# One block for attention and the last stage, with the gating of three images run between the attention's score groups

## The chip, the cores and the metric

The kernel runs on one core of a Trainium2 chip. The metric is the device time of one execution in microseconds (us). Before the change it is 2979.22 us (median of 3 runs, 2973.39 to 2980.7).

## The reference, cut to what matters

Four images (B = 4) of 224 x 224 become 56 x 56 patches and a class token: T = 3137 tokens of 128 features. Attention has 8 heads of 16 features and a relative position bias. It is followed by a layer norm, a gate that picks 2 of 8 experts for each image, and the two chosen experts.

```python
h = _L0_tok_ref(x, W, b, cls)                       # (4, 3137, 128)
h = h + _L0_attn_ref(_layernorm(h), Wq, Wk, Wv, Wo, bias_table)
h = h + _L0_ffn_ref(_layernorm(h), attn_w, attn_b, gate_w, gate_b, w1, b1, w2, b2)

# _L0_ffn_ref
scores = x @ attn_w + attn_b
aw = softmax(scores, axis=1)
pooled = sum(x * aw, axis=1)                        # one row for an image
gates = softmax(pooled @ gate_w + gate_b)
_, idx = top_k(gates, 2)                            # two experts for an image
h = gelu(x @ w1[e] + b1[e]);  eo = gelu(h @ w2[e] + b2[e])
```

## The kernel before, in words

The program is a row of blocks with a barrier between them. Tokens are held transposed (128 features on the partitions) and cut into CH = 8 chunks of W = 393 columns.

**First block.** Projections of all images (lines 398 to 460 on TensorE), up to about 213 us. Then attention, whose order is written out by `fast_order` (line 81). One unit is one tile of 128 keys by 393 queries of one of 32 heads (NBH). A head has two sides of four chunks, and one side is a *pass* of 4 x 25 = 100 units; there are 64 passes and 6400 units. Units are put into groups of 4 and 3 in turn. The even group uses PSUM banks 0 to 3, the odd one banks 4 to 6, and bank 7 takes the output. In `scores(g)` (line 466) TensorE waits until ScalarE has exponentiated group g - 2, then makes the score matmuls of the group in f16 (lines 481 and 484), two units beside each other on the rows of the array. ScalarE turns a whole group into exponentials with one instruction (line 575). POOL multiplies the part of a tile near the diagonal by the exponentiated bias (line 620). In `values(m)` (line 487) TensorE multiplies a batch of four units by the value rows in f32 (line 507), four units beside each other on the columns; a batch is issued four groups or more behind its scores and waits for POOL's products. At the end of a pass VectorE copies the output out of bank 7 (line 692), shuffles, takes the reciprocal (697) and multiplies (700). SP stores that half head (line 347), and loads the head after next.

**Second block.** A fallback for large scores, guarded by a flag that every engine loads (lines 819, 909, 927, 1011, 1037). It is skipped with these inputs.

**Third block, the last stage.** Weights are loaded (lines 1263 to 1265), then `gating` runs for each image: output projection (line 1360, the matmul called Y in the change), mean (1340, M), variance (1333, V), square root on ScalarE (1412), reciprocal on VectorE (1472), product (1474), pooling score (1352, S), maximum (1479), exponential (1420), weighted sum (1485), gate logits (1364, G), and the choice of two experts in small VectorE steps. Then `experts` runs 16 units for each image (chunk by expert): four matmuls into the hidden layer (line 1376), Gelu (1436), four matmuls out of it (1384), Gelu (1444), and the weighted add on VectorE (1540). The gating of the next images is laid between the expert units of the current one, from a distance of five slots. Image 0's gating has nothing beside it but the first slots of image 1's. SP loads attention chunks (1273) and expert weights, POOL stores the output (1316).

```python
for g in range(NG + DELAY + 2):
    if g < NG:
        scores(g)
    while done < NB and group_of[batches[done][-1]] + (done % KT == 0) <= g - DELAY - AHEAD:
        values(done)
        done += 1
```

Of the kernel before, what the change touches and what calls it, by code (L numbers as in the profile page):

```python
# [8 lines left out]
F32 = mybir.dt.float32  # L9
# [11 lines left out]
CH = 8  # L21
# [5 lines left out]
REACH = 91  # L27
GMAX = 4
# [29 lines left out]
def at(count):  # L58

    return count + 1  # L60
# [20 lines left out]
def fast_order(NBH, KT):  # L81

    units = [(n, kt, 4 * side + c) for n in range(NBH) for side in range(2) for kt in range(KT) for c in range(4)]
    groups, u = [], 0
    while u < len(units):
        size = GMAX - len(groups) % 2
        groups.append(list(range(u, min(u + size, len(units)))))
        u += size
    batches = [list(range(m, m + 4)) for m in range(0, len(units), 4)]
    return units, groups, batches  # L90


def build(nc, B, S, d):
# [22 lines left out]
    wide_rows = nc.dram_tensor("wide_rows", (HEADS, WIDE), F32, kind="Internal")  # L116
    att_rows = nc.dram_tensor("att_rows", (NBH, CH, 32, W), F32, kind="Internal")

    top = ExitStack()
    with top:  # L120
# [5 lines left out]

        to_prime = []

        def primed(ctx, name, start=1):

            s = semaphore(ctx, name)
            to_prime.append((s, start))
            return s
# [16 lines left out]
        with ctx:  # L152
# [21 lines left out]
            qk_sq = sbuf(ctx, "qk_sq", [P, 2, 2, W], BF16)  # L174
            halves = sbuf(ctx, "halves", [P, 2, 2, 2, W], F16)
# [8 lines left out]
            s_load = semaphore(ctx, "s_load")  # L184
            s_x = [semaphore(ctx, f"s_x{b}") for b in range(B)]
            s_set = semaphore(ctx, "s_set")
            s_h_mm = semaphore(ctx, "s_h_mm")
            s_h = primed(ctx, "s_h")
            s_xc_mm = semaphore(ctx, "s_xc_mm")
            s_wc = semaphore(ctx, "s_wc")  # L190
            s_hsel = semaphore(ctx, "s_hsel")
            s_n2 = semaphore(ctx, "s_n2")
            s_n2k = semaphore(ctx, "s_n2k")
            s_xc = primed(ctx, "s_xc")
            s_sq = semaphore(ctx, "s_sq")
            s_var = semaphore(ctx, "s_var")
            s_std = primed(ctx, "s_std")
            s_rstd = semaphore(ctx, "s_rstd")
            s_ln = primed(ctx, "s_ln")
            s_qk_mm = semaphore(ctx, "s_qk_mm")  # L200
            s_qk_sq = semaphore(ctx, "s_qk_sq")
            s_hi = semaphore(ctx, "s_hi")
            s_lo = primed(ctx, "s_lo")
            s_ln_out = primed(ctx, "s_ln_out")
            s_norm_mm = primed(ctx, "s_norm_mm")
            s_norm = primed(ctx, "s_norm")
            s_v_mm = primed(ctx, "s_v_mm")
            s_v = primed(ctx, "s_v")
            s_v_out = [semaphore(ctx, f"s_v_out{b}") for b in range(B)]
            s_parts_out = [[semaphore(ctx, f"s_parts_out{b}_{i}") for i in range(2)] for b in range(B)]  # L210
            s_band_mm = semaphore(ctx, "s_band_mm")
            s_band = semaphore(ctx, "s_band")
            s_right = semaphore(ctx, "s_right")
            s_shift = semaphore(ctx, "s_shift")
            s_init_out = semaphore(ctx, "s_init_out")
            s_chain = semaphore(ctx, "s_chain")
            s_fl = semaphore(ctx, "s_fl")
            s_fl_mm = semaphore(ctx, "s_fl_mm")
# [44 lines left out]
            s_init = semaphore(ctx, "f_init")  # L263
            s_toep = semaphore(ctx, "f_toep")
            s_e = semaphore(ctx, "f_e")
            s_tick = semaphore(ctx, "f_tick")
            s_ld = [semaphore(ctx, f"f_ld{i}") for i in range(2)]
            s_vld = [semaphore(ctx, f"f_vld{i}") for i in range(2)]
            s_score = semaphore(ctx, "f_score")
            s_exp = semaphore(ctx, "f_exp")  # L270
            s_biased = semaphore(ctx, "f_band")
            s_pv = primed(ctx, "f_pv", BATCHES)
            s_o = primed(ctx, "f_o")
            s_shuf = semaphore(ctx, "f_shuf")
            s_inv = semaphore(ctx, "f_inv")
            s_norm_o = semaphore(ctx, "f_norm_o")
            s_o_out = [primed(ctx, f"f_o_out{i}") for i in range(2)]
# [6 lines left out]
            units, groups, batches = fast_order(NBH, KT)  # L284
# [23 lines left out]
            def batches_until(g):  # L308

                return batch_of[groups[g][-1]] + 1  # L310

# [3 lines left out]
            def _(sp):  # L315
# [78 lines left out]
                for b in range(B):  # L394
                    sp.wait_ge(s_v_out[b], 16)
                    for i in range(2):
                        sp.wait_ge(s_parts_out[b][i], CH * 16)
                for n in range(NBH):
                    store_half(n, 0)
# [4 lines left out]
                for side in range(2):  # L404
                    sp.wait_ge(s_o_out[side], at(16 * NBH))

            @blk.tensor
            def _(pe):
# [57 lines left out]
                def scores(g):  # L466

                    if g >= AHEAD:
                        pe.wait_ge(s_exp, g - AHEAD + 1)
                    for j, u in enumerate(groups[g]):  # L470
# [15 lines left out]
                    last.then_inc(s_score, 1)  # L486

# [24 lines left out]
                for g in range(NG + DELAY + 2):  # L512
                    if g < NG:
                        scores(g)
                    while done < NB and group_of[batches[done][-1]] + (done % KT == 0) <= g - DELAY - AHEAD:
                        values(done)
                        done += 1
                while done < NB:
                    values(done)
                    done += 1  # L520

            @blk.scalar
            def _(act):
# [42 lines left out]

                act.wait_ge(s_toep, 16)
                nc.scalar.activation(e_all[:], e_all[:], ACT.Exp).then_inc(s_e, 1)
                for g in range(NG):
                    act.wait_ge(s_score, g + 1)  # L570
                    if g >= SLOTS_PR:
# [4 lines left out]
                                         ACT.Exp, scale=1.0 / (LIFT * LIFT)).then_inc(s_exp, 1)  # L576

            @blk.gpsimd
            def _(pool):
# [31 lines left out]

                pool.wait_ge(s_e, 1)
                for u in banded:
# [6 lines left out]
                    nc.gpsimd.tensor_tensor(p, p, e_all[0:keys, n % HEADS, t:t + z - a], ALU.mult).then_inc(s_biased, 1)  # L620

            @blk.vector
            def _(dve):
# [63 lines left out]
                for k in range(NBH // 2):  # L687
                    for half in range(4):
                        side = half % 2
                        drained = 4 * k + half  # L690
                        dve.wait_ge(s_pv, BATCHES + k * BATCHES + KT * (half + 1))
                        nc.vector.tensor_copy(o_sb[:, side], ps[:, O_PS, 0:W]).then_inc(s_o, 1)  # L692
                        dve.wait_ge(s_o, at(drained + 1))
                        nc.vector.tensor_copy(tick[:, 0:1], o_sb[:, side, 0:1]).then_inc(s_tick, 1)
                        nc.vector.stream_shuffle(inv[:, side], o_sb[:, side], [HD + i % HD for i in range(32)]).then_inc(s_shuf, 1)
                        dve.wait_ge(s_shuf, drained + 1)
                        nc.vector.reciprocal(inv[:, side], inv[:, side]).then_inc(s_inv, 1)  # L697
                        dve.wait_ge(s_inv, drained + 1)
                        dve.wait_ge(s_o_out[side], at(16 * (2 * k + half // 2)))
                        nc.vector.tensor_tensor(o_norm[:, side], o_sb[:, side], inv[:, side], ALU.mult).then_inc(s_norm_o, 1)  # L700
# [3 lines left out]
        with ctx:  # L704
# [37 lines left out]
            wide_sb = sbuf(early, "z_wide_sb", [HEADS, WIDE])  # L742
            early.close()

# [73 lines left out]
            def _(sp):  # L818
                flag = sp.value_load(flag_i[0:1, 0:1], min_val=0, max_val=3 * HEADS)
                with sp.If(flag > 0):  # L820
                    for dst, src in ((wq2, "Wq"), (wk2, "Wk")):
# [3 lines left out]
                    sp.wait_ge(s_zero2, 1)  # L825
# [81 lines left out]
            def _(pool):  # L907
                prime(pool)
                flag = pool.value_load(flag_i[0:1, 0:1], min_val=0, max_val=3 * HEADS)
                with pool.If(flag > 0):  # L910
                    nc.gpsimd.memset(qg[:, TP:KT * P], 0.0).then_inc(s_pad, 1)
# [14 lines left out]
            def _(pe):  # L926
                flag = pe.value_load(flag_i[0:1, 0:1], min_val=0, max_val=3 * HEADS)
                with pe.If(flag > 0):
                    pe.wait_ge(s_set2, 1)
# [80 lines left out]
            def _(act):  # L1010
                flag = act.value_load(flag_i[0:1, 0:1], min_val=0, max_val=3 * HEADS)
                with act.If(flag > 0):
                    with act.Fori(0, CHUNKS) as n:
# [22 lines left out]
            def _(dve):  # L1036
                flag = dve.value_load(flag_i[0:1, 0:1], min_val=0, max_val=3 * HEADS)
                with dve.If(flag > 0):
                    nc.vector.memset(shift_sb[:, 0:3], 0.0).then_inc(s_zero2, 1)
                    dve.wait_ge(s_w2, 48)  # L1040
# [8 lines left out]
                    with dve.Fori(0, CHUNKS) as n:  # L1049
                        dve.wait_ge(s_zero2, 1)  # L1050
# [98 lines left out]
        with ctx:  # L1149
            wo = sbuf(ctx, "wo", [P, P])  # L1150
            pool_w = sbuf(ctx, "pool_w", [P, 1])
            pool_wr = sbuf(ctx, "pool_wr", [P, P])
            pool_b = sbuf(ctx, "pool_b", [P, 1])
            gate_w = sbuf(ctx, "gate_w", [P, E])
# [426 lines left out]
```

## Time and profile before

| what | us |
|---|---|
| median of the runs (range) | 2979.22 (2973.39 to 2980.7) |
| the profiled execution's own time | 2981.47 |
| its span | 2979.8 |
| projections, until attention's first exponential | 213 |
| attention, first to last exponential (L575) | 2252 |
| from there to the end of the span | 515 |
| mean granted TensorE clock | 0.977 |

PE is TensorE, PEld its weight load, DVE VectorE, ACT ScalarE, SP the queue of most transfers. The table's stages come from the first and last starts of line 575. A row of the timeline gives start, duration, line and operation; "x8" means eight instructions merged, and each f32 matmul of the program leaves two records of MATMUL. Ends of matmuls are modelled, so the distance between two starts is a better measure than a duration. PEclk and "clock" are the granted clock as a share of 2.4 GHz.

### The profile page before, as it was taken

To read this page: it belongs to the slowest core of one execution; us is meant where nothing else is said; L and a number is where in the kernel's file an instruction comes from. 1 tells how busy PE (TensorE), PEld (TensorE's weight loads), DVE (VectorE), ACT (ScalarE), POOL (GpSimd) and SP (SyncE) were. 2 spreads that over 40 slices of the span, in tenths; PEclk is the share of its full clock that TensorE was granted. 3 is DMA by queue.
4 is the path that set the end of the run, shared out by engine and by line. 5 is a ranking of instruction groups with operands and counts; after the bars stand their busy time and mean duration, and the time that the engine had idled before them with its cause. 6 is when DMAs were issued, how large, how long until landed. Compare 5 with 4: busy or idle time off the path is not lost. (4 is left out here: it accounts for less than half of the span.)

```text
span 2979.8 us, 53098 instructions
## 1 busy us (share of the span) xinstructions
PE 2783.5 (93%) x21844; PEld 959.2 (32%) x21844; DVE 633.0 (21%) x798; ACT 2637.8 (89%) x2520; POOL 760.7 (26%) x1421
## 2 busy tenths in 40 slices
PE   7989999999999999999999999999999994799998
PEld 3442222222222222222222222222222221455555
DVE  4751111111111111111111111111111114555441
ACT  4769999999999999999999999999999992467664
POOL 2213332222222333333333322222223330000000
PEclk8989999999999999999999999999999997799999
DMA  5540100000000000000010000000000001110110
GB/s 132 173 156 13 33 29 29 26 26 26 26 28 27 26 26 26 26 26 26 31 34 29 30 29 27 26 26 26 29 26 26 26 7 38 41 42 22 42 33 19
DMA packets 64755, 111.18 MB, mean 37 GB/s; under 512 B 9938, under 2 KB 55084, under 8 KB 63796
## 3 DMA queue, kind: packets, MB, share of 16 engines
q1 hardware_dynamic: 62460, 101.27, 10.9%
q0 software_dynamic: 2048, 6.43, 0.6%
q8 instruction: 178, 2.92, 0.4%
q14 instruction: 69, 0.57, 0.1%
HBM read 62.47 MB, written 46.48 MB: 37 GB/s over the span
## 5 line engine op out<-in xcount | busy, mean ns | idle before, releaser
L575 ACT ACTIVATE shared<-ps 128x1572 f32<-128x1572 f32 (+1 forms) x1829 | 2231.8, 1343 | 20.0 <-PE ps L484 10.0
L507 PE MATMUL ps<-shared,va 128*32 128x393 f32 x12800 | 1433.5, 523 | 0.2 <-DVE flag_i L685 0.2
L620 POOL TENSOR_TENSOR shared<-shared,e_all 128x310 f32<-128x310 f32 (+19 forms) x1344 | 703.5, 537 | 1556.8 <-ACT shared L575 1552.3
L484 PE MATMUL ps<-qa,ka 48*128 48x393 f16 (+7 forms) x3808 | 625.8, 319 | 49.3 <-ACT shared L575 47.3
L481 PE MATMUL ps<-qa,ka 51*128 51x393 f16 (+18 forms) x3360 | 564.5, 314 | 46.5 <-ACT shared L575 45.9
L507 PEld LDWEIGHTS ps<-shared,va 128*32 128x32 f32 x12800 | 360.0, 149 | 459.9 <-issue 440.6
L692 DVE COPY xc<-ps 128x393 f32<-128x393 f32 x64 | 36.4, 568 | 1961.4 <-PE ps L507 1961.4
L484 PEld LDWEIGHTS ps<-qa,ka 48*128 48x128 f16 x3808 | 184.2, 95 | 571.4 <-ACT shared L575 469.5
L481 PEld LDWEIGHTS ps<-qa,ka 51*128 51x128 f16 (+1 forms) x3360 | 151.7, 95 | 600.0 <-ACT shared L575 568.8
L1376 PE MATMUL ps<-ln_all,w 128*128 128x393 f32 x512 | 180.1, 494 | 4.9 <-ACT hid L1436 4.9
L1436 ACT ACTIVATE hid<-ps,b 128x393 f32<-128x393 f32 x256 | 135.3, 587 | 54.7 <-PE ps L1376 54.2
L1384 PE MATMUL ps<-hid,w 128*128 128x393 f32 x512 | 180.0, 493 | 1.5 <-ACT eo L1444 1.5
L697 DVE RECIPROCAL sq<-sq 128x393 f32<-128x393 f32 x64 | 167.3, 2615 | 2.2
L1316 POOL DMA_DIRECT2D out<-h_all x32 | 17.5, 546 | 476.6 <-DVE h_all L1540 476.6
L1376 PEld LDWEIGHTS ps<-ln_all,w 128*128 128x128 f32 x512 | 96.4, 190 | 78.5 <-ACT hid L1436 9.1
L1384 PEld LDWEIGHTS ps<-hid,w 128*128 128x128 f32 x512 | 97.0, 190 | 74.3 <-issue 2.7
L1444 ACT ACTIVATE eo<-ps,b 128x393 f32<-128x393 f32 x64 | 37.9, 592 | 89.2 <-PE ps L1384 89.2
L653 DVE RECIPROCAL std<-std 128x393 f32<-128x393 f32 x32 | 83.7, 2614 | 33.7 <-ACT std L532 33.7
L1472 DVE RECIPROCAL dev<-dev 128x393 f32<-128x393 f32 x32 | 83.4, 2608 | 12.1 <-ACT dev L1412 12.1
L1540 DVE SCALAR_TENSOR_TENSOR h_all<-eo,gsc,h_all 128x393 f32<-128x393 f32 x64 | 40.1, 627 | 170.6 <-ACT eo L1444 170.1
L608 POOL TENSOR_TENSOR ln<-xc,std 128x393 f32<-128x393 f32 x32 | 32.6, 1017 | 163.7 <-DVE std L653 136.9
L542 ACT ACTIVATE qk_sq<-ps 128x786 bf16<-128x786 f32 x32 | 26.4, 827 | 51.1 <-PE ps L429 30.2
(118 smaller groups left out, 942.9 us busy)
## 6 DMA issues: line engine op xcount, KB each, us to landing
qa<-q_halves SPq DMA_DIRECT2D x64, 196.5 KB
ka<-k_halves SPq DMA_DIRECT2D x64, 196.5 KB
att_rows<-std SPq DMA_DIRECT2D x64, 196.5 KB, 2.4
v_rows<-v_sb SPq DMA_DIRECT2D x4, 1600.0 KB, 6.7
va<-v_rows SPq DMA_DIRECT2D x32, 200.0 KB, 16.1
ln_rows<-ln SPq DMA_DIRECT2D x32, 196.5 KB, 5.5
q_halves<-halves SPq DMA_DIRECT2D x32, 196.5 KB, 3.1
k_halves<-halves SPq DMA_DIRECT2D x32, 196.5 KB, 4.3
```

The costliest lines, as they stand in the source:

```text
L481: last = nc.tensor.matmul(out[:, 0:cut], ka[r:r + 51, par, k0:k0 + keys], qa[r:r + 51, par, q0:q0 + cut], start=True, stop=True, tile_posi ...
L484: last = nc.tensor.matmul(out[:, cut:W], ka[r:r + 48, par, k0:k0 + keys], qa[r:r + 48, par, q0 + cut:q0 + W], start=True, stop=True, tile_ ...
L507: last = nc.tensor.matmul(ps[quad:quad + 32, O_PS, 0:W], va[0:keys, par, :, kt], pr[0:keys, g % SLOTS_PR, j], start=(kt == 0), stop=(kt == ...
L575: nc.scalar.activation(pr[:, g % SLOTS_PR, 0:m], ps[:, b0:b0 + m, 0:W], ACT.Exp, scale=1.0 / (LIFT * LIFT)).then_inc(s_exp, 1)
L620: nc.gpsimd.tensor_tensor(p, p, e_all[0:keys, n % HEADS, t:t + z - a], ALU.mult).then_inc(s_biased, 1)
L653: nc.vector.reciprocal(std[:, c % 2], std[:, c % 2]).then_inc(s_rstd, 1)
L697: nc.vector.reciprocal(inv[:, side], inv[:, side]).then_inc(s_inv, 1)
L1376: last = nc.tensor.matmul(ps[:, HID_PS + sl:HID_PS + sl + 1, 0:W], w1[:, 2 * par + e, sl * P:(sl + 1) * P], ln_all[:, bass.ds(b, 1), c * W ...
L1384: last = nc.tensor.matmul(ps[:, EO_PS, 0:W], w2[:, 2 * par + e, sl], hid[:, (s - 1) % 2, sl], start=(sl == 0), stop=(sl == HS - 1))
L1436: last = nc.scalar.activation(hid[:, s % 2, sl], ps[:, HID_PS + sl, 0:W], ACT.Gelu, bias=b1[:, 2 * par + e, sl:sl + 1])
L1472: nc.vector.reciprocal(v, v).then_inc(s_rstd, 1)
L1540: nc.vector.scalar_tensor_tensor(h, eo[:, u % 2], gsc[:, e:e + 1], h, ALU.mult, ALU.add).then_inc(s_acc, 1)
```

## The change

The third block is copied into the first one, so that attention and the experts have no barrier between them. The old third block stays only behind the fallback's flag, and the fallback recomputes h. Semaphores are kept over all blocks.

- `fast_order` now lists 33 *guests* for each of images 0 to 2: 8 each of Y, M, V, S, and one G. Three stand in a pass, at units 35, 58 and 80, from the second pass of the next image's heads on, and G in its pass 14. A guest takes the fourth bank of an even group, which shrinks from 4 units to 3. TensorE issues it in `visit` right after the group's scores, and `scores(g + 2)` waits until VectorE has emptied the bank.
- VectorE receives each guest in `receive`, in one hand-written order with the drains, the maximum, the pooled sum and the choice.
- The inverse root is no longer a square root on ScalarE and a reciprocal on VectorE, but `rstd`: a shift and exclusive or on the bits, then three Newton steps of three VectorE instructions each, and the product.
- ScalarE makes images 0 to 2's two exponentials of the gating between attention groups.
- SP loads attention chunks, writes and reloads the normed images (1.6 MB each) and loads expert weights within its attention order.
- The experts of all four images follow attention as 64 units without a loop, with two alternating banks for the second product. Image 3's gating is laid in as one guest after each of units 3 to 34 (`LATE`), its exponentials at units 36 and 39, its choice at 40.

```diff
+    for b in range(B - 1):
+        q = 2 * HEADS * (b + 1)
+        places += [(q + 1 + i // 3) * PASS + (35, 58, 80)[i % 3] for i in range(4 * CH)] + [(q + 14) * PASS + 58]
     while u < len(units):
         size = GMAX - len(groups) % 2
+        if size == GMAX and len(guest_at) < len(places) and u >= places[len(guest_at)]:
+            guest_at[len(groups)] = len(guest_at)
+            size = GMAX - 1
...
                     if g >= AHEAD:
                         pe.wait_ge(s_exp, g - AHEAD + 1)
+                    if g - AHEAD in guest_at:
+                        pe.wait_ge(s_guest, guest_at[g - AHEAD] + 1)
...
+                def visit(k, bank):
+                    b, kind, c = guest(k)
+                    if kind == "Y":
+                        pe.wait_ge(s_att[c % 4], 16 * (b * CH // 4 + c // 4 + 1))
+                        weight, moving, n = wo[:], att[:, c % 4], W
...
+                    elif kind == "S":
+                        pe.wait_ge(s_ln2, b * CH + c + 1)
+                        weight, moving, n = pool_wr[:], x2[b][:, x], W
+                    else:
+                        pe.wait_ge(s_pooled, b + 1)
+                        weight, moving, n = pooled[:], gate_w[:], E
+                    if k > 0:
+                        pe.wait_ge(s_guest, k)
+                    nc.tensor.matmul(ps[:, bank, 0:n], weight, moving, start=True, stop=True).then_inc(s_guest_mm, 1)
...
                     if g < NG:
                         scores(g)
+                    if g in guest_at:
+                        visit(guest_at[g], GUEST_PS)
...
+                pe.wait_ge(s_exp, NG)
+                pe.wait_ge(s_guest, (B - 1) * GUESTS)
+                for U in range(B * NU + 1):
+                    experts(U)
+                    if U in LATE:
+                        visit(LATE[U], LATE_PS)
...
+                    if g in pool_exp_at:
+                        pool_exp(pool_exp_at[g])
+                    if g in gate_exp_at:
+                        gate_exp(gate_exp_at[g])
...
+                def rstd(b, c, x):
+                    v, y, t = root[:, 0], root[:, 1], root[:, 2]
+                    r0 = (b * CH + c) * 9
+                    nc.vector.tensor_scalar(y.bitcast(I32), v.bitcast(I32), 1, HALF_BITS,
+                                            ALU.logical_shift_right, ALU.bitwise_xor).then_inc(s_root, 1)
+                    scale = ROOT
+                    for i in range(3):
+                        dve.wait_ge(s_root, r0 + 3 * i + 1)
+                        nc.vector.scalar_tensor_tensor(t, y, scale * scale, v, ALU.mult, ALU.mult).then_inc(s_root, 1)
+                        dve.wait_ge(s_root, r0 + 3 * i + 2)
+                        nc.vector.tensor_tensor(t, t, y, ALU.mult).then_inc(s_root, 1)
+                        dve.wait_ge(s_root, r0 + 3 * i + 3)
+                        if i < 2:
+                            nc.vector.scalar_tensor_tensor(y, t, -3.0, y, ALU.add, ALU.mult).then_inc(s_root, 1)
+                        else:
+                            nc.vector.scalar_tensor_tensor(t, t, -3.0, y, ALU.add, ALU.mult).then_inc(s_rstd2, 1)
+                        scale = -scale / 2
+                    dve.wait_ge(s_rstd2, b * CH + c + 1)
+                    nc.vector.scalar_tensor_tensor(x2[b][:, x], t, scale, x2[b][:, x], ALU.mult, ALU.mult).then_inc(s_ln2, 1)
...
+                for g in range(NG + 4):
+                    if g in guest_at:
+                        receive(guest_at[g], GUEST_PS)
+                    if g in drain_at:
+                        drain(drain_at[g])
...
             @blk.sync
             def _(sp):
-                for dst, src in ((wo, "Wo"), (pool_w, "attn_w"), (gate_w, "gate_w")):
...
+                flag = sp.value_load(flag_i[0:1, 0:1], min_val=0, max_val=3 * HEADS)
+                with sp.If(flag > 0):
```

## Rows read from the trace of the kernel before

**Rows 1.** The page, section 1: busy time, share and instructions of each engine.

```profile
PE 2783.5 (93%) x21844; PEld 959.2 (32%) x21844; DVE 633.0 (21%) x798; ACT 2637.8 (89%) x2520; POOL 760.7 (26%) x1421
```

**Rows 2.** Windows by stage: length, busy time of each engine, PEclk, DMA, GB/s.

```profile
224.00:2466.00 2242.00, 2149.84 (x19910) 621.07 (x19910) 279.70 (x378) 2222.35 (x1822) 698.73 (x1336) 1.00 0.08 26
2467.00:2570.00 103.00, 48.58 (x95) 19.98 (x96) 52.86 (x73) 24.31 (x38) 0.15 (x1) 0.69 0.15 45
2570.00:2880.00 310.00, 304.34 (x921) 173.29 (x921) 154.25 (x207) 208.83 (x346) 12.19 (x23) 1.00 0.11 35
```

**Rows 3.** Lines by shape, attention stage: count, busy us, mean ns, idle before.

```profile
L575 ACT ACTIVATE shared<-ps 128x1572 f32<-128x1572 f32 x910 | 1369.9, 1505 | 9.2 <-PE ps L484 3.2
L575 ACT ACTIVATE shared<-ps 128x1179 f32<-128x1179 f32 x911 | 1076.6, 1182 | 9.5 <-PE ps L484 6.9
```

**Rows 4.** Timeline of attention, PE: start us, us, line and operation.

```profile
956.49 0.51 PE L484 MATMUL ps<-qa,ka 48*128 48x393 f16 x3
...
956.93 0.90 PE L507 MATMUL ps<-shared,va 65*32 65x393 f32 x8
...
957.76 0.51 PE L484 MATMUL ps<-qa,ka 48*128 48x393 f16 x4
...
958.44 0.50 PE L484 MATMUL ps<-qa,ka 48*128 48x393 f16 x3 [0.17 <-ACT shared L575]
...
958.88 0.90 PE L507 MATMUL ps<-shared,va 128*32 128x393 f32 x8
...
959.85 0.51 PE L484 MATMUL ps<-qa,ka 48*128 48x393 f16 x4
```

**Rows 5.** Timeline, from the last attention work to the first expert matmul.

```profile
2465.62 1.19 PE L507 MATMUL ps<-shared,va 128*32 128x393 f32 x12
...
2471.42 0.33 SPq L347 DMA_DIRECT2D att_rows<-std  x1
2479.83 0.36 SPq L1263 DMA_DIRECT2D wo<-in_Wo  x1
...
2490.26 1.65 PE L1360 MATMUL ps<-att,wo 128*128 128x393 f32 x2 [23.44 <-DMA att<-att_rows]
...
2567.84 2.80 PE L1376 MATMUL ps<-ln_all,w 128*128 128x393 f32 x8
```

**Rows 6.** The page, section 6: issues, KB each, median us to landing.

```profile
att_rows<-std SPq DMA_DIRECT2D x64, 196.5 KB, 2.4
```

**Rows 7.** Timeline of the last image's experts, PE alone working.

```profile
2902.68 2.81 PE L1384 MATMUL ps<-hid,w 128*128 128x393 f32 x8
...
2907.97 2.81 PE L1384 MATMUL ps<-hid,w 128*128 128x393 f32 x8
```

**Rows 8.** Timeline around a pooling exponential in the last stage.

```profile
2639.43 2.91 ACT L1420 ACTIVATE sc<-sc,st 128x3137 f32<-128x3137 f32 x1
...
2644.86 2.91 PE L1376 MATMUL ps<-ln_all,w 128*128 128x393 f32 x8 [1.43 <-ACT hid L1436]
```

**Rows 9.** Timeline, the last expert matmuls.

```profile
2969.70 2.88 PE L1384 MATMUL ps<-hid,w 128*128 128x393 f32 x8 [0.77 <-ACT eo L1444]
```

**Rows 10.** Lines of the last stage: VectorE steps and a table load.

```profile
L1540 DVE SCALAR_TENSOR_TENSOR h_all<-eo,gsc,h_all 128x393 f32<-128x393 f32 x64 | 40.1, 627 | 170.6 <-ACT eo L1444 170.1
...
L1474 DVE TENSOR_TENSOR ln_all<-xc,dev 128x393 f32<-128x393 f32 x32 | 18.2, 569 | 1.1
...
L1479 DVE TENSOR_REDUCE st<-sc 128x1 f32<-128x3137 f32 x4 | 13.7, 3421 | 12.4 <-ACT sc L1416 12.4
...
L1420 ACT ACT_TABLE_LOAD x4 | 5.1, 1283 | 0.1
```

**Rows 11.** One shape on POOL, all of attention, then one in 0.7 us.

```profile
L620 POOL TENSOR_TENSOR shared<-shared,e_all 128x73 f32<-128x73 f32 x32 | 13.0, 405 | 6.3 <-ACT shared L575 6.3
...
L620 POOL TENSOR_TENSOR shared<-shared,e_all 128x73 f32<-128x73 f32 x1 | 0.8, 754 | 0.0
```

**Rows 12.** Timeline of DVE in that stretch.

```profile
997.00 0.57 DVE L700 TENSOR_TENSOR std<-xc,sq 128x393 f32<-128x393 f32 x1
```

More of the change, by code:

```diff
@@ L125, in semaphore, with primed @@
             return ctx.enter_context(nc.semaphore(name))
+        held = ExitStack()
+        top.enter_context(held)
+        spare = []
         to_prime = []
-        def primed(ctx, name, start=1):
-            s = semaphore(ctx, name)
+        def primed(ctx, name=None, start=1):
+            s = semaphore(ctx, name) if ctx else spare.pop()
             to_prime.append((s, start))
@@ L206, in build @@
[L206 to L218, printed above, removed]
+            s_load = semaphore(held, "s_load")
+            s_x = [semaphore(held, f"s_x{b}") for b in range(B)]
+            s_set = semaphore(held, "s_set")
+            s_h_mm = semaphore(held, "s_h_mm")
+            s_h = primed(held, "s_h")
+            s_xc_mm = semaphore(held, "s_xc_mm")
+            s_wc = semaphore(held, "s_wc")
@@ L272, in build @@
[L272 to L277, printed above, removed]
+            wo = sbuf(ctx, "wo", [P, P])
+            pool_w = sbuf(ctx, "pool_w", [P, 1])
+            pool_wr = sbuf(ctx, "pool_wr", [P, P])
+            pool_b = sbuf(ctx, "pool_b", [P, 1])
+            gate_w = sbuf(ctx, "gate_w", [P, E])
@@ new lines, in build @@
+            s_w3 = semaphore(held, "f_w3")
+            s_set3 = semaphore(held, "f_set3")
+            s_att = [semaphore(held, f"f_att{i}") for i in range(4)]
+            s_guest_mm = semaphore(held, "f_guest_mm")
+            s_guest = semaphore(held, "f_guest")
+            s_sq2 = semaphore(held, "f_sq2")
+            s_root = semaphore(held, "f_root")
+            s_rstd2 = semaphore(held, "f_rstd2")
+            s_ln2 = semaphore(held, "f_ln2")
+            s_top = semaphore(held, "f_top")
@@ new lines, in build, with guest, guest_number, expert_unit @@
+            GUEST_PS, LATE_PS, HID_PS, EO_PS = 3, 6, 0, 4
+            GUESTS = 4 * CH + 1
+            EW = 16 * 8
+            NU = 2 * CH
+            GATE_OPS = 15
+            guest_list = guest_order()
+            def guest(k):
+                return (k // GUESTS,) + guest_list[k % GUESTS]
+            def guest_number(b, kind, c):
+                return b * GUESTS + guest_list.index((kind, c))
+            def expert_unit(U):
+                return U // NU, U % NU // 2, U % 2
+            LATE = {3 + i: (B - 1) * GUESTS + i for i in range(4 * CH)}
@@ L282, in build @@
             DELAY = 2
-            units, groups, batches = fast_order(NBH, KT)
+            units, groups, batches, guest_at = fast_order(B, KT)
             NG = len(groups)
@@ new lines, in _ @@
+                for U in range(1, B * NU + 1):
+                    b, c, e = expert_unit(U - 1)
+                    if (U - 1) % NU == 0:
+                        dve.wait_ge(s_gsc, b + 1)
+                    dve.wait_ge(s_eo, at(U))
+                    dve.wait_ge(s_acc, at(U - 1))
+                    h = h_all[:, b, c * W:(c + 1) * W]
+                    nc.vector.scalar_tensor_tensor(h, eo[:, (U - 1) % 2], gsc[:, b, e:e + 1], h, ALU.mult, ALU.add).then_inc(s_acc, 1)
+                    if U in LATE:
+                        receive(LATE[U], LATE_PS)
+                    if U == LATE_MAX:
+                        pool_max(B - 1)
+                    if U == LATE_POOL:
+                        pool_sum(B - 1)
+                    if U == LATE_PICK:
+                        pick_two(B - 1)
@@ L928, in _ @@
                 with pe.If(flag > 0):
+                    for b in range(B):
+                        pe.wait_ge(s_x2, 48 + 32 * (b + 1))
+                        for c in range(CH):
+                            pe.wait_ge(s_h2_copy, b * CH + c + 1)
+                            nc.tensor.matmul(ps[:, 6 + c % 2, 0:W], w_again[:], x_again[:, c * W:(c + 1) * W], start=True, stop=True).then_inc(s_h2_mm, 1)
                     pe.wait_ge(s_set2, 1)
```

992 lines of the change are left out of this document (647 added, 345 removed).

## The prediction

> **What bounds the kernel now.** The page [rows 1] has PE at 93% and ACT at 89%, which says nothing about who is waiting for whom, so I read the stages next [rows 2]. In attention ACT is busy 2222 of 2242 us, and PE 2150. The lines by shape [rows 3] show ACT idle for only 19 us before its 1821 exponentials: attention is bound by ACT. The two shapes differ by 0.323 us for one unit. A group takes 2242 / 1822 = 1.23 us and holds 3.5 units, so a group costs about 0.10 us beyond its units.
>
> The question for this change is how much PE has to spare there. By starts [rows 4] a score phase takes 0.44 us (956.49 to 956.93), whether it holds 3 or 4 units, and a batch of values 0.83 us (956.93 to 957.76). Two groups are 7 units: two score phases and 1.75 batches, 0.88 + 1.45 = 2.33 us, against 2.46 us of ACT. That is 0.13 us spare, or 1.8 us in a pass (100 units, 14.3 such pairs). Seen as waits it is less: after two score phases in a row (every eighth group) PE waits 0.24 us between them (0.68 - 0.44) and 0.14 us after the batch (0.97 - 0.83), 0.38 us in 8 groups, 1.4 us in a pass. So PE has 1.4 to 1.8 us in a pass of 35 us.
>
> After attention nothing of this kind runs beside anything else. The last values start at 2465.62 and end at 2466.8, and the first expert matmul starts at 2567.84 [rows 5]: 101 us, in which PE is busy less than half of the time at a granted clock of 0.69 [rows 2]. From then on PE bounds: one expert unit takes 5.29 us (2902.68 to 2907.97), 16 records of 0.33 us without a gap [rows 7].
>
> **The new tail, from the end of the last values to the end.** The span now has 2979.8 - 2466.8 = 513.0 us there. I build the new one from rows:
> - 64 units x 5.29 = 338.6 us. The first matmuls need weights and normed tokens that SP fetches during the last head, on DMA engines that are 8% busy [rows 2]; if they were late, their few us would stand here.
> - Image 3's 32 visits of two records each, 32 x 0.66 = 21.1 us, and 0.5 for G. All are on PE's path. The inputs were received on VectorE some units before, and SP's chunk loads for them wait for the last drain (last store at 2471.42), while the first visit comes three units, 16 us, in. VectorE's Newton chain (7.4 us, below) exceeds one unit with its visit (5.95), but four visits need 0.57 + 1.14 + 7.4 + 0.57 and four adds 2.5 us, 12.2 of 23.8, and `eo` has two buffers.
> - Start-up, with the Gelu table load of 1.28 us [rows 10] partly beside the first matmuls: 1.0. The last second product waits for the last Gelu: 0.8 [rows 9].
> - The pooling exponential at unit 36. Before, such a place left PE idle for 1.43 us, with other matmuls of the gating to fill in [rows 8]. Now ACT also waits, in its order, for the add and the maximum, 0.63 + 3.42 us [rows 10], then 3.1 for the exponential and its sum, then 1.28 for the table and 1.1 for the first two Gelus: 9.5 to 9.7 us after its last one; PE has matmuls for 4.5 of them: 5.2 us of stall. The gate exponential at 39 is short: 0.3. Small waits around visits, taken as 1.7.
> - After the last matmul: 2979.8 - 2972.6 = 7.2 us as now [rows 9].
> - A skipped block. From the last store's issue to the first load behind the skipped fallback are 8.4 us (2471.42 to 2479.83); 2.4 of them are the store's landing [rows 6], so a skipped block costs 6.0. The end now has two instead of none: 12.0.
> Together 388.4 us, so the tail gives back 124.6.
>
> **What attention pays.**
> - Guests on PE. 33 passes hold three guests (32 guests of an image in 11 passes, three images). A guest is two records, 0.66 us by [rows 7], and I take 0.70 for the change between tilings. The shrunken groups make (100 + 3) / 3.5 - 100 / 3.5 = 0.86 more score phases, 0.44 each. So 2.1 + 0.4 = 2.5 us more on PE, against 1.4 to 1.8 to spare: PE becomes the bound of these passes, by 0.9 us each. 33 x 0.9 = 30 us. Bounds: 20 us if the waits around drains serve too, 82 if none of PE's slack can be used at the place where the guest stands (99 x 0.70 + 28 x 0.44). I am near the lower end, since guests stand 22 to 55 units apart and the spare time collects at each double score phase. ACT's own part of the extra groups (28 x 0.10) lies beneath.
> - ACT's own additions, with no cover since ACT bounds those passes: three exponentials of 3137 columns, 2.91 us each [rows 8], with reading of the sum and the two small ones about 3.7: 11 us. Exp is already loaded.
> - VectorE. It is busy 280 of 2242 us, so load is no matter, order is. The chain of `rstd`, priced by [rows 10]: six two-input steps and the product of 0.627, three products of 0.569, the first step from PSUM 0.56. The shift step has no row; it is bounded by 0.15 (the small steps' size) and 0.63, I take 0.4. With 0.03 taken between two steps, 7.4 us. Behind it stand the next guest's receive (22 units, 7.7 us later, plus 2.4 us until `scores(g + 2)` needs the bank) and, after a guest at unit 80, the drain, due some 11 us later. Both fit, so nothing. Maximum and pooled sum (3.4 us each) stand alone at unit 50.
> - SP: 24 chunk loads, three stores and one reload of 1.6 MB and eight expert loads are issued between head loads that are two heads early. Its waits are for guests received a pass before. Nothing. POOL's queue gets the output stores only behind its last product.
> - POOL. It works 699 us in attention, nearly all in the half of a pass that meets the diagonal: about 62% there. A product of 128x73 takes 405 ns on average, but 754 ns where it ran beside VectorE's two-input product [rows 11, 12]: during 0.55 us of overlap it advanced by about a quarter of its pace. `rstd` has ten such steps, 6.2 us. About 2 chains of 8 fall wholly, 3 partly into POOL's half. Whole ones leave POOL 1.9 us behind, while values are issued some 1.6 us after a product is normally ready. I count 5 us in all; bounds 0 and 51 (15 chains x 3.4).
> The Trainium skill (GPSIMD Engine Reference, Key points) states this as a rule: POOL shares its SBUF interfaces with VectorE and contends with VectorE steps that have two SBUF inputs. The trace agrees, with its 754 against 405 ns. It speaks against putting Newton steps beside POOL's products, and is rival 3.
>
> Attention pays 30 + 11 + 5 = 46 us.
>
> **Sum.** 2979.8 - 124.6 + 46 = 2901 us of span. The profiled execution took 2981.5 and the median is 2979.2, 0.6 below this span, so I say 2901 for the median as well. The change, 2.6%, is far over the 0.3% that a measurement of this kernel can tell.
>
> **Rivals.**
> 1. *PE's slack cannot be used* (chance 0.15). A guest delays the next scores by 0.7 us, ACT starves at once, and the batch order keeps PE from catching up. For it: at each batch PE runs at 1.27 us for a group against ACT's 1.23, so it has a cushion only after a double score phase. Against: a full eighth group of cushion follows. Price 82 instead of 30: 2953.
> 2. *More is hidden than I count* (0.12). The reserve takes all but 20 us, POOL costs nothing, and the stall at unit 36 halves: 2901 - 10 - 5 - 3 = 2883, down to 2870 if blocks skip in half the time as well.
> 3. *POOL becomes the bound while `rstd` runs* (0.12). PE waits in `values` for products, 1.9 to 3.4 us in 15 chains: 28 to 51 us instead of 5, 2924 to 2947.
> 4. *Slower: the chain on VectorE holds the bank* (0.05). `scores(g + 2)` waits for the receive, and that stands behind `rstd` in VectorE's order. It decides once a chain exceeds 9.5 us; each further us costs 24 us. It takes 79 us more to reach the old time, so a chain of 12.8 us, 1.07 us for a step. Speaks against it: steps of 0.57 and 0.63, and the product beside POOL also took 0.57. At 13.5 us it gives 2997.
> The change does what it says in any case, since blocks and order are written by hand.
>
> The forecast has 0.56; its own range is 2885 to 2920. The range of 2868 to 2942 adds most of rivals 2 and 3 and leaves out rival 1's end, rival 4 and the tails. Faster 0.94, same 0.01, slower 0.05.
>
> **What would show it.** In the profile after: expert units 5.29 us apart from start to start; the first expert matmul within 3 us of the last values; PE's hole at unit 36 about 5 us; passes with guests near 36.1 us and passes without at 35.2; idle time of ACT behind PE's score lines grown to about 30 us; no score line waiting for VectorE. A `rstd` of over 9.5 us, or many waits of L507 for POOL, would prove me wrong, and so would a tail over 400 us.

## The result, and the profile after

The changed kernel takes 3006.99 us (median of 4 runs, 3005.91 to 3009.41), against 2976.3 us for the kernel before in the same session: a ratio of 1.0096, with a 95% interval of 1.0083 to 1.0109. It is slower by 1%, where I forecast 2901 us and 2.6% faster. The profiled execution spans 3004.3 us. One execution of the kernel before in a later session ran at a mean clock of 0.748 and took 3386.07 us; it is left out of every median below.

The page, sections 1 and 2 (the row of [rows 1], and the busy share and the clock in 40 slices of the span):

```profile
PE 2819.5 (94%) x21844; PEld 955.0 (32%) x21844; DVE 805.6 (27%) x1182; ACT 2574.9 (86%) x2422; POOL 779.8 (26%) x1421
...
ACT  4669999999998999999989999999989999844553
...
PEclk9989999999999999999999999999999999999999
```

PE's share went up and ACT's went down, in a kernel that ACT bounded for three quarters of its time. The hole of the clock at the start of the last stage (0.69 in [rows 2]) is gone, and in ACT's row slices with an 8 have come up inside attention. Attention by windows, as in [rows 2] (the row ends with attention's last exponentials; columns as there):

```profile
224.00:2614.00 2390.00, 2265.76 (x20046) 654.11 (x20042) 547.85 (x837) 2251.07 (x1859) 713.92 (x1330) 0.98 0.09 30
```

and the lines by shape in the same stage, to be read against [rows 3]:

```profile
L824 ACT ACTIVATE shared<-ps 128x1572 f32<-128x1572 f32 x824 | 1238.3, 1503 | 31.2 <-PE ps L664 14.7
L824 ACT ACTIVATE shared<-ps 128x1179 f32<-128x1179 f32 x1023 | 1189.8, 1176 | 107.8 <-PE ps L661 60.1 <-PE ps L664 44.9
```

Line 824 is line 575 of before, 661 and 664 are the scores 481 and 484. The exponentials have the same durations. What is new is idle time in front of them, 139.0 us against 18.7, and it stands before the groups of three, behind PE. From the start of its first exponential to the end of its last, attention runs from 209.8 to 2615.1 us: 2405.3 us against 2251.8 (213.2 to 2465.0), so it pays 153 us. I had counted 46.

The tail went as forecast. The handover, in the timeline:

```profile
2613.52 3.54 PE L738 MATMUL ps<-shared,va 128*32 128x393 f32 x40
...
2616.99 2.91 PE L707 MATMUL ps<-ln,v_sb 128*128 128x393 f32 x8
...
2618.66 1.28 ACT L842 ACT_TABLE_LOAD   x1 [3.56 <-PE ps L707]
...
2621.07 2.91 PE L707 MATMUL ps<-ln,v_sb 128*128 128x393 f32 x8 [1.18 <-ACT qa L842]
```

The first expert matmul starts where the last value matmul ends; before, 101 us lay between them [rows 5]. From 2617.1 to 3004.3 are 387 us; the prediction's new tail was 388.4 us, against 513.0 before.

A guest, 0.86 us between two phases that used to follow each other (832.44 scores, 832.88 guest, 833.74 values), and what ACT does then:

```profile
832.88 0.93 PE L691 MATMUL ps<-halves,wo 128*128 128x393 f32 x2
...
833.74 0.90 PE L738 MATMUL ps<-shared,va 128*32 128x393 f32 x8
833.84 0.57 DVE L994 TENSOR_TENSOR h_all<-h_all,ps 128x393 f32<-128x393 f32 x1 [10.02 <-PE ps L691]
...
834.57 0.34 PE L664 MATMUL ps<-qa,ka 48*128 48x393 f16 x2
...
835.11 7.28 ACT L824 ACTIVATE shared<-ps 128x1179 f32<-128x1179 f32 x6 [0.76 <-PE ps L661]
...
837.93 0.34 PE L661 MATMUL ps<-qa,ka 51*128 51x393 f16 x2 [0.31 <-ACT shared L824]
```

ACT is idle for 0.76 us at once. Three microseconds later PE waits 0.31 us for ACT at its double score phase, as it did before the change. So the spare time of PE is still there after the guest, unused. It is so over all passes: in the traces PE's idle time adds up to 1.50 us in a pass before, and to 2.18 us in the 30 passes that hold three guests now, 0.5 of which are waits for a chunk, shown next.

And in each of the three images once, at the fifth output projection:

```profile
952.62 1.68 PE L691 MATMUL ps<-halves,wo 128*128 128x393 f32 x2 [5.15 <-DMA halves<-att_rows]
...
956.55 7.04 ACT L824 ACTIVATE shared<-ps 128x1179 f32<-128x1179 f32 x6 [7.78 <-PE ps L661]
```

The load that PE waits for was issued only at 936.34, behind two things in SP's queue: a wait that lasted until 929.85, and the pieces of a head:

```profile
895.75 0.34 SPq L466 DMA_DIRECT2D att_rows<-std  x1
929.85 1.07 SPq L455 DMA_DIRECT2D qa<-q_halves  x2
...
936.34 4.30 SPq L530 DMA_DIRECT2D halves<-att_rows  x2
```

The wait also costs clock. The window from 949.5 to 956.3 us has a granted clock of 0.50, the lower of its two levels; with the chunk loads first (below) no such stretch lies here:

```profile
949.50:956.30 6.80, 3.68 (x14) 1.00 (x16) 0.57 (x1) 0.00 (x0) 0.00 (x0) 0.50 0.09 31
```

### The profile page after: what moved, and what is told of

Its sections match the earlier page's. It is cut to its first block, busy times and chain, and to the rows that moved or that the text cites. A ratio compares the mean times of both kernels' runs of the same rounds, so it can differ in the third digit from the quotient of the medians.

```text
span 3004.3 us, 53203 instructions
## 1 busy us (share of the span) xinstructions
PE 2819.5 (94%) x21844; PEld 955.0 (32%) x21844; DVE 805.6 (27%) x1182; ACT 2574.9 (86%) x2422; POOL 779.8 (26%) x1421
## 4 chain that ended last, share of the span: by engine, by line
PE 43%; ACT 34%; issue 16%; DMA 4%; DVE 1%; SPq 1%; POOL 0%; ACTq 0%; POOLq 0%
ACT shared L824 34%; PE ps L738 16%; PE ps L664 6%; PE ps L707 6%; PE ps L715 6%; PE ps L661 5%; PE ps L691 3%; DMA halves<-att_rows 2%; DMA k_halves<-halves 1%; PE ps L607 1%; DVE std L939 0%; PE ps L601 0%; PE ps L622 0%; DMA band_rows<-band_sb 0%; SPq L455 0%
## 5 line engine op out<-in xcount | busy, mean ns | idle before, releaser
L824 ACT ACTIVATE shared<-ps 128x1572 f32<-128x1572 f32 (+1 forms) x1857 | 2256.3, 1322 | 140.4 <-PE ps L661 61.3
L900 POOL TENSOR_TENSOR shared<-shared,e_all 128x310 f32<-128x310 f32 (+19 forms) x1344 | 722.2, 550 | 1691.4 <-ACT shared L824 1686.2
L664 PE MATMUL ps<-qa,ka 48*128 48x393 f16 (+12 forms) x3808 | 634.2, 320 | 52.6 <-ACT shared L824 49.9
L842 ACT ACTIVATE qa<-ps,b 128x393 f32<-128x393 f32 x256 | 136.5, 586 | 82.6 <-PE ps L707 82.6
L849 ACT ACTIVATE ka<-ps,b 128x393 f32<-128x393 f32 x64 | 37.8, 590 | 98.3 <-PE ps L715 98.3
L1102 DVE SCALAR_TENSOR_TENSOR h_all<-ka,gsc,h_all 128x393 f32<-128x393 f32 x64 | 40.2, 628 | 242.9 <-ACT ka L849 242.9
L715 PE MATMUL ps<-qa,v_sb 128*128 128x393 f32 x256 | 89.9, 493 | 0.0
L715 PE MATMUL ps<-qa,e_all 128*128 128x393 f32 x256 | 89.7, 493 | 0.0
L707 PE MATMUL ps<-shared,e_all 128*128 128x393 f32 x256 | 89.7, 493 | 0.0
L994 DVE TENSOR_TENSOR h_all<-h_all,ps 128x393 f32<-128x393 f32 x32 | 18.0, 564 | 182.4 <-PE ps L691 182.4
```

The source lines that it names most:

```text
L664: last = nc.tensor.matmul(out[:, cut:W], ka[r:r + 48, par, k0:k0 + keys], qa[r:r + 48, par, q0 + cut:q0 + W], start=True, stop=True, tile_ ...
L707: last = nc.tensor.matmul(ps[:, HID_PS + sl, 0:W], w1[b % 2][:, e, sl * P:(sl + 1) * P], ln2[b][:, c * W:(c + 1) * W], start=True, stop=True)
L715: last = nc.tensor.matmul(ps[:, EO_PS + U % 2, 0:W], w2[b % 2][:, e, sl], hid[:, (U - 1) % 2, sl], start=(sl == 0), stop=(sl == HS - 1))
L824: nc.scalar.activation(pr[:, g % SLOTS_PR, 0:m], ps[:, b0:b0 + m, 0:W], ACT.Exp, scale=1.0 / (LIFT * LIFT)).then_inc(s_exp, 1)
L842: last = nc.scalar.activation(hid[:, U % 2, sl], ps[:, HID_PS + sl, 0:W], ACT.Gelu, bias=b1[:, 2 * (b % 2) + e, sl:sl + 1])
L1102: nc.vector.scalar_tensor_tensor(h, eo[:, (U - 1) % 2], gsc[:, b, e:e + 1], h, ALU.mult, ALU.add).then_inc(s_acc, 1)
```

## The experiments

Theory A: a guest stalls ACT at once, because PE needs 0.86 us more and the shrunken group gives ACT 0.33 us less. Its rival B: the loss comes through VectorE, from the receives, the Newton chain and POOL's delay. C: the granted clock of TensorE. All kernels have three rounds against the kernel before, which took 2980.7, 2980.2 and 2979.6 us in the three sessions. The changed kernel itself was measured in an earlier session, in which the kernel before took 2976.3 us, so a difference between it and a variant can be off by some 5 us. Where that matters I also give the length of attention in the profiled executions; it is free of the projections, whose end alone moved between 203 and 213 us in the eleven traces.

**Smaller groups alone.** The kernel before, with `fast_order` of the change; nothing uses the free bank.

```diff
         size = GMAX - len(groups) % 2
+        if size == GMAX and len(guest_at) < len(places) and u >= places[len(guest_at)]:
+            guest_at[len(groups)] = len(guest_at)
+            size = GMAX - 1
```

> The kernel before, with the 99 shrunken even groups of the change and nothing in their fourth bank: 28 more groups. Theory A (a guest stalls ACT at once: 0.86 us more on PE, and a group that is a unit, 0.33 us, shorter on ACT) expects the shorter group alone to cost little: 3 us for the groups, at most 20 us where the cushion is under 0.33 us. Theory B (the waits for VectorE, its Newton steps and POOL's delay behind them make the loss) expects 3 us. Theory C (the granted clock of TensorE dips more often in the changed attention) expects 3 us and the 5 or 6 short dips of before.

Measured: 3000.58 us, ratio 1.006 (1.0042 to 1.0078), 20 us over before (25.0 by the length of attention). That is the upper end of A, over the 3 us of B and C. 28 groups more at 0.10 us are 3; the last run below shows where the other 17 come from.

**The matmuls alone.** The same, with an unread matmul in the free bank.

```diff
                     if g < NG:
                         scores(g)
+                    if g in guest_at:
+                        nc.tensor.matmul(ps[:, 3, 0:W], mean_w[:], h_all[:, 0, 0:W], start=True, stop=True)
```

> The kernel before, with the shrunken groups and a f32 matmul of 128x128 by 393 columns in the free bank at all 99 places. Nobody reads it, nobody waits for it, and VectorE and SP do what they did. Theory A expects nearly the whole loss of attention here: 99 x 1.05 = 104 us more than before. Theory B expects the 30 us of the prediction, since PE's spare time absorbs the rest. Theory C expects, over A or B, about 12 more dips of 3 to 10 us and 30 us from them if the matmuls themselves bring the dips, and no more dips if waits do.

Measured: 3090.84 us, ratio 1.0366 (1.0347 to 1.0384), 110 us over before. Its lines by shape, in attention up to 2370 us (over the whole of it, to 2569 us, the two idle times add up to 108.5):

```profile
L586 ACT ACTIVATE shared<-ps 128x1572 f32<-128x1572 f32 x749 | 1126.1, 1504 | 24.1 <-PE ps L493 8.2
L586 ACT ACTIVATE shared<-ps 128x1179 f32<-128x1179 f32 x937 | 1090.3, 1177 | 77.5 <-PE ps L490 38.0 <-PE ps L493 36.9
```

No VectorE step, transfer or wait of the change is in this kernel, and ACT has most of the idle time of the changed kernel, before the same groups. 99 matmuls cost 90 us over the smaller groups, 0.91 us each, no less than the 0.86 us that one of them holds PE: nothing of them was hidden. Of these 90 us, 82 appear in the trace right at the 99 shrunken groups, as a longer distance from their exponential to the next. B falls as the main cause. So does C: it wanted about 12 more stretches of low clock from the matmuls, and there are three more (9, 31 us long in all, against 6 and 20 us).

**Chunk loads first.**

```diff
                     store_half(n, 0)
-                    if n + 2 < NBH:
-                        sp.wait_ge(s_o, at(2 * n + 2))
-                        load_head(n + 2)
                     if b >= 0 and into == 1:
                         load_attention(b, 4)
                         load_attention(b, 5)
                     if b >= 0 and into == 2:
                         load_attention(b, 6)
                         load_attention(b, 7)
+                    if n + 2 < NBH:
+                        sp.wait_ge(s_o, at(2 * n + 2))
+                        load_head(n + 2)
```

> The changed kernel, with SP's loads of chunks 4 to 7 ahead of the load of the head after next instead of behind it. The trace has PE waiting for chunk 4 once in each of three images, 7 to 8 us of ACT idle each. All theories expect 20 to 24 us less than the changed kernel; theory C also expects the dips that follow these waits to go, up to 10 us more.

Measured: 2980.96 us, ratio 0.9998 (0.9989 to 1.0008), 26 us under the changed kernel; attention is 21.9 us shorter in the trace. That is the 20 to 24 expected, within what two sessions can tell. In the changed kernel the chunk stood in SP's order behind a wait for a drain at the end of that pass and behind eleven pieces of a head. Now it follows the store at once:

```profile
895.92 0.34 SPq L466 DMA_DIRECT2D att_rows<-std  x1
896.31 1.37 SPq L530 DMA_DIRECT2D halves<-att_rows  x2
```

**Without Newton steps.** This leaves out the nine instructions of each inverse root.

```diff
-                    for i in range(3):
...
+                    dve.wait_ge(s_root, b * CH + c + 1)
+                    nc.vector.scalar_tensor_tensor(x2[b][:, x], y, ROOT, x2[b][:, x], ALU.mult, ALU.mult).then_inc(s_ln2, 1)
```

> The changed kernel without the nine Newton instructions of each inverse root: the first guess from the bit pattern is used as it is. That leaves out VectorE work of 32 x 9 steps, 5.4 us for a chunk. Theory A expects no change (0 to -5 us). Theory B expects 15 us less or more, up to 60, as POOL and the receives behind the chain come free.

Measured: 2999.19 us (its four runs lie between 2994 and 3005), ratio 1.0061 (1.0037 to 1.0086), 8 us under the changed kernel. Of the 10.3 us between the spans of the two profiled executions, 4.5 lie in attention, 1.6 in the tail, and 4.2 before attention, where the two kernels are the same. That fits A's 0 to 5, and is under the 15 that B needed.

**One item behind a score phase, on the matmuls alone.**

```diff
+                    room = 1
                     if g in guest_at:
                         nc.tensor.matmul(ps[:, 3, 0:W], mean_w[:], h_all[:, 0, 0:W], start=True, stop=True)
+                        room = 0
-                    while done < NB and group_of[batches[done][-1]] + (done % KT == 0) <= g - DELAY - AHEAD:
+                    while done < NB and group_of[batches[done][-1]] + (done % KT == 0) <= g - DELAY - AHEAD and (
+                            room > 0 or group_of[batches[done][-1]] <= g - DELAY - AHEAD - 3):
                         values(done)
                         done += 1
+                        room -= 1
```

> The kernel before with the shrunken groups and the 99 unread matmuls, as in the run of matmuls alone (110 us over before), but TensorE issues at most one item behind a group's scores: either the matmul or one batch of values. The batch that gives way moves on by one group until a group without a batch absorbs it. Theory A says that the loss comes from 0.86 us put on top of a full 1.27 us between two score phases. In a guest pass PE then needs 25 x 0.83 + 3 x 0.86 + 29.43 x 0.44 = 36.3 us against 35.05 now: 33 x 1.25 = 41 us over before instead of 110, 60 at most. If the loss were something that a full-width f32 matmul does to its neighbours wherever it stands, it stays near 110.

Measured: 3039.54 us, ratio 1.0202 (1.0185 to 1.0219), 59 us over before instead of 110. The same matmuls at the same groups cost about half as much when a batch gives way to them, so the loss is not something that such a matmul does to its neighbours wherever it stands. That is A's mechanism, at the upper end of its range. The traces show what happened to PE's spare time. A pass is taken here from the start of its first exponential to that of the next pass, and PE's idle time is the sum of the gaps before its matmuls:

| kernel | pass without a guest: us, PE idle | pass with three: us, PE idle |
|---|---|---|
| before | 35.2, 1.5 | |
| matmuls alone | 35.5, 1.6 | 38.4, 1.65 |
| matmuls alone, one item | 35.2, 1.3 | 37.1, 0.5 |

With one item the guests use most of the spare time, and PE works through 36.5 of 37.1 us. So PE itself now bounds these passes, at a little over the 36.3 us of the sum above, and what remains of the loss is mostly its load.

**The changed kernel with both mends.** Chunk loads first and one item.

> The changed kernel with SP's chunk loads first, and with at most one item (guest or batch) behind a group's scores. Theory A expects 50 to 70 us less than with the chunk loads first alone (2981), so 2911 to 2931. If the receives on VectorE or the bank held by the guest matter, less than 20 us are gained.

Measured: 2927.4 us, ratio 0.9834 (0.9815 to 0.9854), inside the range of 2911 to 2931. It beats both kernels, the one before by 53 us and the changed one by 80, of which 26 are the chunk loads and 54 the one item. If VectorE's receives or the held bank were what costs, less than 20 would have been gained. A guest in its timeline, with no batch beside it:

```profile
1038.42 0.91 PE L738 MATMUL ps<-shared,va 128*32 128x393 f32 x8
...
1039.27 0.51 PE L664 MATMUL ps<-qa,ka 48*128 48x393 f16 x3
...
1039.70 0.93 PE L691 MATMUL ps<-halves,wo 128*128 128x393 f32 x2
...
1040.56 0.50 PE L664 MATMUL ps<-qa,ka 48*128 48x393 f16 x3
...
1040.99 0.90 PE L738 MATMUL ps<-shared,va 128*32 128x393 f32 x8
```

From scores to scores are 1.29 us (1039.27 to 1040.56), as with a batch (1.27), not 2.13 (832.44 to 834.57). ACT's idle time, by shape:

```profile
L828 ACT ACTIVATE shared<-ps 128x1572 f32<-128x1572 f32 x823 | 1235.1, 1501 | 23.6 <-PE ps L664 5.6 <-PE ps L661 0.5
L828 ACT ACTIVATE shared<-ps 128x1179 f32<-128x1179 f32 x1022 | 1192.4, 1172 | 17.8 <-PE ps L664 5.8 <-PE ps L661 0.3
```

41.4 us, against 139.0. Attention itself fell by less, from 2405.3 to 2328.5 us, because the idle column shows only stalls in which ACT stands still. Neighbouring exponentials overlap by about 0.12 us when ACT always has its next group ready, and a delay shorter than that shows in no idle time. Counted by their starts, exponentials late by less than 0.3 us cost 59 us in the changed kernel and 111 here; those late by more cost 155 and 25 (44 and 17 in the kernel before). The single stalls are gone, and a thin spread of small delays in PE-bound passes has taken the place of a part of them.

**Guests spread over 13 passes.**

```diff
-        places += [(q + 1 + i // 3) * PASS + (35, 58, 80)[i % 3] for i in range(4 * CH)] + [(q + 14) * PASS + 58]
+        spots = [(p, x) for p in range(1, 14) for x in ((35, 58, 80) if p % 2 and p < 12 else (35, 80))]
+        places += [(q + p) * PASS + x for p, x in spots] + [(q + 15) * PASS + 20]
```

> As the one-item version, with the 32 guests of an image over 13 passes, two or three in each, instead of three in each of 11, and the pooling moments moved back by up to 1.5 passes. A pass with two guests needs 35.3 us of PE by the same sum, hardly over ACT's, so theory A expects 12 us less than the one-item version; at most 5 us less if what remains are single stalls at guests, whose number stays.

Measured: 2926.07 us, ratio 0.9826 (0.9809 to 0.9843), 1.3 us less. A miss for the 12 us, within the 5 of the other reading: the rest of the loss goes with the number of guests, not with how full a pass is. In the trace a pass takes 35.6 us without a guest, 36.5 with two and 37.3 with three. The sum gave 35.3 for two guests and counted on PE filling its last gap; it still idles 0.8 us there.

**One item, in the kernel before and with the smaller groups.** The same rule without guests.

> The kernel before with at most one batch of values behind a group's scores, nothing else. Theory A puts the 22 stalls of 0.2 us and more at pass ends down to two batches in one group; it expects 5 to 15 us less than before. If those stalls come from the drain of the output bank, no change.

Measured: 2973.76 us, ratio 0.9981 (0.9971 to 0.9991), 6 us less than before, at the lower end of the 5 to 15 expected.

> The kernel before with the shrunken groups and the rule of one batch for a group. With the old rule the shrunken groups alone cost 20 us. Theory A splits that into 12 us of PE that 28 more score phases need, which stays, and doubled batches that the smaller groups can no longer cover, which go: 0 to 12 us over before. If two groups of 3 in a row are themselves the loss (2.09 us of ACT against 2.54 of PE), it stays at 15 to 20 us.

Measured: 2996.71 us, ratio 1.0058 (1.0035 to 1.0081), 17 us over before, and 23 over the kernel before with the same rule. Doubled batches are not the cause, then, and the 0 to 12 of theory A is missed; the second reading, 15 to 20, holds. So the cost of the shrunken groups is their shape: ACT is through with two groups of three in 2.09 us, and PE needs 2.54 for what belongs to them. In the traces at least 21 of the 23 us lie at these two groups, the shrunken one and the one behind it. That their number stays the same is at least a part of the miss of the spread version; how large a part was not tried.

## Why the prediction was wrong

**What bounds, and the tail: right.** 387 us against 388.4, and not by luck of cancelling terms: from the first expert matmul to the last are 369 us (forecast 369.2), from there to the end 18.6 (forecast 19.2, the two skipped blocks included). The hole at the pooling exponential was foreseen with 5.2 us:

```profile
2843.05 5.01 PE L707 MATMUL ps<-shared,v_sb 128*128 128x393 f32 x8 [4.99 <-ACT qa L842]
```

The 125 us that the tail was to give back are there. They were given away again in attention, and more.

**The step that failed: guests on PE, 30 us.** I took PE's spare time of a pass, 1.4 to 1.8 us, and set 2.5 us of guests against it, since "the spare time collects at each double score phase". The amount was right (1.50 in the trace), but a guest's delay reaches ACT before the next double score phase comes, and the spare time cannot be moved to where a guest stands. Passes with three guests (30 of them, with 3 of two, and not 33) were to take 36.1 us and take 39.3. PE's order is written out, and ACT has scores for one group beyond the one it works on. A guest put on top of a full score-and-batch pair makes the next scores 0.86 us late, ACT starves at once, and when PE comes to its double score phase it waits for ACT as ever. Measured in its place: 20 us for the smaller groups and 90 us for the matmuls, 110 us in all, where I had 30. This was rival 1, to which I gave 0.15. Its price of 82 was low in two terms: a guest costs 0.91 us and not 0.70 (21 us), and the smaller groups 20 instead of 12.

**SP: nothing. Wrong by 22 to 26 us.** I looked at which guest a chunk load waits for, but not at the wait for the drain and the head load queued ahead of it.

**ACT's own additions, 11 us: right.** In attention they show as

```profile
L809 ACT ACTIVATE v_sb<-v_sb,st 128x3137 f32<-128x3137 f32 x3 | 8.8, 2946 | 0.0
L814 ACT ACTIVATE gt<-gt,st 128x8 f32<-128x8 f32 x3 | 1.0, 340 | 0.0
L814 ACT ACTIVATION_READ_ACCUMULATOR gt<-gt,st 128x1 f32 x3 | 0.7, 241 | 0.0
L809 ACT ACTIVATION_READ_ACCUMULATOR v_sb<-v_sb,st 128x1 f32 x3 | 0.7, 231 | 0.0
```

together 11.2 us.

**VectorE and POOL: the time right, the durations only away from POOL.** Where POOL rests, the chain takes 7.0 us (forecast 7.4), every step 0.57 and the unpriced shift 0.37:

```profile
880.63 0.57 DVE L1002 TENSOR_SCALAR root<-ps 128x393 f32<-128x393 f32 x1 [8.92 <-PE ps L691]
881.23 0.37 DVE L1019 TENSOR_SCALAR root<-root 128x393 int32<-128x393 int32 x1
...
887.06 0.57 DVE L1034 SCALAR_TENSOR_TENSOR ln<-root,ln 128x393 f32<-128x393 f32 x1
```

But 14 of the 24 chains in attention take longer, up to 9.72 us, because beside POOL's products VectorE slows down as well. I had priced only POOL's side of it, from one product of VectorE that kept its 0.57 us beside POOL. In the slowest chain:

```profile
1704.18 2.07 POOL L900 TENSOR_TENSOR shared<-shared,e_all 65x156 f32<-65x156 f32 x3 [1.58 <-ACT shared L824]
1704.27 1.39 DVE L1026 TENSOR_TENSOR root<-root 128x393 f32<-128x393 f32 x1
```

That chain is over the 9.5 us that I had named as a sign of being wrong, and yet no score or value matmul waits for VectorE or POOL in the waits of this trace: rivals 3 and 4 did not come. Without the Newton steps attention is 4.5 us shorter, where I took 5 for POOL.

The parts add up: 20 + 90 + 26 + 8 + 11 = 155 us by the medians, and 25.0 + 89.6 + 21.9 + 4.5 + 11.2 = 152 us by the lengths of attention in the traces, against 153 measured there. The tail gave back 126 (513 to 387), and attention began 3 us earlier, which lies within the spread of its beginning over all traces. The spans, 3004.3 and 2979.8, lie 24.5 us apart, the medians 31, since the profiled execution of before took 2981.5 us itself, 5 above its median. With one item behind a score phase 59 us remain, of which the smaller groups are 17 and the rest mostly PE's load. Whether other places for the guests would lower that was not tried.

## What to carry to other kernels

Spare time of an engine in an in-order pipeline has a place. Before work is laid into it, find the wait in which it shows, and put the work there in place of something, so that no stretch between two hand-overs grows; a share of idle time in a stage says nothing of what a single 0.9 us insertion costs. And when a load is queued on a busy DMA issuer, read the waits of everything ahead of it, not only its own.

## What the runs showed of the hardware

A full 128x128 f32 matmul of 393 columns takes 0.66 us in a stream of its like [rows 7], but 0.86 us between the score matmuls, tiled by rows, and the value matmuls, tiled by columns (832.88 to 833.74). Whether the change of tiling makes the difference was not tried.

VectorE steps with two SBUF inputs and POOL's products slow each other down. For POOL it was 754 against 405 ns [rows 11]. A 128x393 step of `rstd` takes 0.57 us alone; over all of attention the mean of one such line is 0.64 us, and the longest single step shown above takes 1.39:

```profile
L1026 DVE TENSOR_TENSOR root<-root 128x393 f32<-128x393 f32 x72 | 46.0, 639 | 2.5
```

TensorE's granted clock in attention is 1.00 for most of the time and 0.5 in short stretches. These add up to 20 us before, 31 with the unread matmuls, 55 with the chunk loads first, 82 in the changed kernel, and 20 in the one-item run of unread matmuls. What they cost can be bounded from the exponentials that begin from 2 us before to 4 us behind such a stretch. Their distances exceed the usual ones by 12 us in all before, 14 with the unread matmuls, 24 with the chunk loads first, and 32 in the changed kernel, part of whose stretches follow a wait for a chunk. So theory C explains at most 20 of the 153 us, those waits included, and almost nothing of the 110 us of the unread matmuls.
